# Polynomial attention with 32-row score tiles, lifted scores, a masked diagonal and overlapped units

## Chip, cores and metric

The program runs on one core of one Trainium2 chip. The metric is the device time of one execution, in microseconds (us). The engines are named as in the profile: PE (TensorE matmul), PEld (its weight loads), DVE (VectorE), ACT (ScalarE), POOL (GpSimd), SP.

## What is computed

Two "macaron" layers run over x of shape 4 x 1024 x 128: mixture-of-experts, attention, mixture-of-experts, FFN in one form, then softmax attention and another FFN. The change touches the first attention alone, which has 16 heads of 8 features, a causal mask and, in place of softmax, a polynomial of each score:

```python
qkv = x @ W_attn
att = einsum('bhid,bhjd->bhij', q, k) / sqrt(8)
# for i >= j:  att > 0: (att**2 + 1) / 1000;  -100 <= att <= 0: (1 - 0.01*att) / 1000;  below -100: 0
y = einsum('bhij,bhjd->bhid', polymax(att), v)
x = x + y.reshape(B, T, C) @ W_proj
```

## The kernel before

`macaron` (L2019) runs its phases one after another. Each is a block in which every engine has its own program and waits on semaphores. `attn0_phase` (L886) is the phase that changes.

**Loops.** Batch elements b (4) and in each 4 groups g of 4 heads; m = 4b + g counts the 16 groups. `pipeline` (L976) has each engine do `attend` for group m with `prepare` for group m + 1 threaded in between, so that ten units u of scores alternate with ten steps k of preparation. The loop over the first three elements is a loop on the chip; the last one is written out.

**Layout.** A head takes a strip of 32 rows (`ROW`). Queries and keys are kept as three-part sums in the rows of a strip (high and low halves), so one product in the reduced float32 form (fp32r) gives the full score. `kM` holds four copies of the keys, each with the rows of the other heads zeroed, so each head's score product runs over all 128 rows (L1079).

**Units.** `key_units` (L1424) gives three units for the first 512 queries and seven for the second: 0 and 3 are on the diagonal (four pieces of 128 columns), 1 and 4 have pieces of 384 and 128, 2 and 5 one of 256, and 6 to 9 one of 512. That makes 18 pieces for each of 4 heads.

**A unit.** TensorE makes the scores of each head in one of four PSUM banks; on the diagonal a further product adds a large negative mask (L1083). ScalarE rectifies each head (L1221) and on the diagonal also writes 1 - 0.01 s into `L` (L1220), which GpSimd masks (L1023). VectorE forms r(r + 0.01) in place (L1335); for head 0 of the last three units ScalarE and GpSimd do so (L1225, L1027). TensorE multiplies by the values, four heads at once in 32-column strips, in full float32 (L1098), then adds `L` (L1106) and, for keys further back, a running sum over keys, `S`, applied to the queries (L1112). ScalarE copies the result out (`copy_out`, L1207).

**Preparation.** k = 0, 1 keys; 2 to 5 keys and values by token (`KV`); 6, 7 queries; 8, 9 the running sum. Products go to two banks in turn (L1057, L1063, L1069). ScalarE takes the low halves (L1195) and masks `kM` (L1203); VectorE writes keys, queries and `KV` (L1284 to L1290), `run` (L1301) and the largest magnitudes of keys and queries (L1308, L1315, L1318). GpSimd then makes `S` in three steps (L1007, L1011, L1014).

**The branch.** At a group's end `correct` (L964) has TensorE, ScalarE and VectorE read a flag and branch: only if a score could be under -100 do they recompute the group. It is not taken with this input. After four groups `finish` projects (L1170) and VectorE adds to x with new statistics (L118 to L133).

What sets the order around the change is this hand-written order of each engine, for TensorE:

```python
for u in range(NU):
    scores(m, g, u)
    nxt(u)                      # prepare(m + 1, ..., u)
    if u >= 1:
        values(m, g, u - 1)
```

## Time and profile before

| what | us |
| --- | --- |
| median of 3 runs (3367.14 to 3372.04) | 3371.26 |
| the profiled execution, its own time | 3360.91 |
| its span on the core | 3359.2 |
| PE, DVE, ACT, POOL busy | 2946.4, 2270.8, 1310.0, 858.1 |
| mean granted TensorE clock, share of full speed | 0.935 |

Rows name line, engine, operation and tiles as "out<-in". A group's row ends with count, busy time, mean ns of one instruction, and the engine's idle time just before these with what ended most of it. Line numbers are those of the kernel before. The chain that ended last covers the last few per cent alone (PE 2%, DVE 1%), so stages are read by stretches of time instead.

### The profile page before, as it was taken

Reading aid. Unit: us, or ns where it says so; the run is one execution under the profiler, and the core shown is the slowest. Engines: PE = TensorE matmul, PEld = TensorE weight load, DVE = VectorE, ACT = ScalarE, POOL = GpSimd, SP = SyncE. Lnnn points to the kernel's source line nnn. Section 1 sums busy time; section 2 is a strip of 40 time slices with the busy share of each in tenths; the row PEclk is TensorE's granted clock in tenths of the full one; section 3 lists DMA queues with packets and bytes.
Section 4 is the critical chain, followed back from the end, with each engine's and each line's share of the span. In section 5 each row is a group of like instructions: output and inputs, shape, how many; then the busy total and the mean of one; then the engine's idle time right before and its main releaser. Section 6 shows DMA issues by size and latency. Waiting matters only on the chain. (4 is left out here: it accounts for less than half of the span.)

```text
span 3359.2 us, 58774 instructions
## 1 busy us (share of the span) xinstructions
PE 2946.4 (88%) x16264; PEld 2055.3 (61%) x16296; DVE 2270.8 (68%) x5642; ACT 1310.0 (39%) x2660; POOL 858.1 (26%) x1265
## 2 busy tenths in 40 slices
PE   5999999777777778777999999787998999999987
PEld 4777777655655556555777777644555455565553
DVE  6777777678778677776777777635555555565633
ACT  2111111156566566652111111133554554545532
POOL 1232323244444444441223232101111111111100
PEclk9999999888889988888999999897999999999988
DMA  3000000000000000002000000000000000000000
GB/s 123 0 0 0 0 0 0 1 2 2 3 2 2 3 2 2 2 2 98 0 0 0 0 0 0 1 0 1 1 2 2 1 1 1 1 1 1 1 1 25
DMA packets 13041, 24.09 MB, mean 7 GB/s; under 512 B 2307, under 2 KB 7683, under 8 KB 12805
## 3 DMA queue, kind: packets, MB, share of 16 engines
q1 hardware_dynamic: 12804, 21.22, 1.9%
q8 instruction: 115, 1.88, 0.2%
q14 instruction: 122, 0.99, 0.1%
HBM read 18.52 MB, written 2.10 MB: 6 GB/s over the span
## 5 line engine op out<-in xcount | busy, mean ns | idle before, releaser
L555 DVE SCALAR_TENSOR_TENSOR moe_acc<-moe_ps,moe_comb,moe_acc 128x512 f32<-128x512 f32 x896 | 662.8, 746 | 173.6 <-PE moe_ps L304 170.1
L1335 DVE SCALAR_TENSOR_TENSOR attn_R<-attn_R 128x512 f32<-128x512 f32 (+1 forms) x592 | 479.0, 865 | 116.3 <-ACT attn_R L1221 116.1
L1941 DVE CUSTOM_DVE_ANT_0 attn_masked<-attn_psm,attn_causal 128x1024 f32<-128x1024 f32 (+7 forms) x512 | 367.6, 755 | 205.2 <-PE attn_psm L1666 201.5
L1845 ACT ACTIVATE attn_probs<-attn_pse 128x512 f32<-128x512 f32 (+1 forms) x640 | 319.7, 552 | 291.3 <-PE attn_pse L1680 290.8
L1221 ACT ACTIVATE attn_R<-attn_ps 128x512 f32<-128x512 f32 (+1 forms) x640 | 322.1, 570 | 75.1 <-PE attn_ps L1079 75.1
L304 PE MATMUL moe_ps<-moe_Wg,moe_xh 128*128 128x512 f32 x1024 | 328.9, 403 | 24.2 <-DVE moe_Wu L501 24.2
L304 PE MATMUL moe_ps<-moe_Wu,moe_xh 128*128 128x512 f32 x1024 | 337.0, 411 | 0.0
L335 PE MATMUL moe_ps<-moe_Wd,moe_ih 128*128 128x512 f32 x1024 | 336.4, 410 | 0.0
L1696 PE MATMUL attn_psy<-attn_probs,attn_V 128*64 128x512 f32 (+3 forms) x1536 | 320.7, 517 | 0.4 <-POOL attn_probs L1601 0.3
L1079 PE MATMUL attn_ps<-attn_qS,attn_kM 128*128 128x128 f32 (+3 forms) x1152 | 259.4, 367 | 46.1 <-issue 42.8
L454 POOL TENSOR_SCALAR moe_part<-consts,moe_pick,moe_prob 128x8 f32<-128x8 f32 x256 | 97.4, 394 | 754.1 <-ACT moe_prob L389 754.1
L1601 POOL TENSOR_SCALAR_AFFINE_SELECT attn_probs<-attn_probs 128x256 f32<-128x256 f32 (+1 forms) x192 | 94.7, 493 | 751.3 <-ACT attn_probs L1845 751.3
L1098 PE MATMUL attn_ps<-attn_R,attn_KV 128*32 128x128 f32 (+3 forms) x2304 | 173.8, 417 | 114.1 <-DVE attn_R L1335 113.3
L1079 PEld LDWEIGHTS attn_ps<-attn_qS,attn_kM 128*128 128x128 f32 x1152 | 205.5, 223 | 110.9 <-issue 61.1
L1680 PE MATMUL attn_pse<-attn_qS,attn_kS 110*128 110x512 f32 (+3 forms) x768 | 232.2, 392 | 23.9 <-ACT attn_probs L1845 15.1
L1023 POOL TENSOR_TENSOR attn_L<-attn_L,attn_small 128x512 f32<-128x512 f32 x128 | 206.0, 1639 | 160.9 <-ACT attn_L L1220 160.9
L304 PEld LDWEIGHTS moe_ps<-moe_Wg,moe_xh 128*128 128x128 f32 x1024 | 194.5, 191 | 73.5 <-issue 27.9
L1680 PEld LDWEIGHTS attn_pse<-attn_qS,attn_kS 110*128 110x128 f32 x768 | 119.5, 193 | 188.3 <-ACT attn_probs L1845 109.2
L388 ACT ACTIVATE moe_prob<-moe_gap 128x2 f32<-128x2 f32 x64 | 13.0, 203 | 548.5 <-DVE moe_gap L546 548.5
L335 PEld LDWEIGHTS moe_ps<-moe_Wd,moe_ih 128*128 128x128 f32 x1024 | 185.1, 191 | 41.5 <-issue 1.1
L304 PEld LDWEIGHTS moe_ps<-moe_Wu,moe_xh 128*128 128x128 f32 x1024 | 187.2, 193 | 36.7
L304 PE MATMUL moe_ps<-moe_Wg,moe_xl 128*128 128x512 f32 x512 | 204.7, 400 | 0.0
(207 smaller groups left out, 5033.0 us busy)
## 6 DMA issues: line engine op xcount, KB each, us to landing
moe_stageg<-in_w_gate SPq DMA_DIRECT2D x8, 512.0 KB, 6.9
moe_stageu<-in_w_up SPq DMA_DIRECT2D x8, 512.0 KB, 7.6
moe_stageg<-in_w_down SPq DMA_DIRECT2D x8, 512.0 KB, 3.6
out<-X SPq DMA_DIRECT2D x1, 2048.0 KB, 8.7
attn_qS<-attn_mh SPq DMA_DIRECT2D x64, 4.0 KB
attn_qS<-attn_ml SPq DMA_DIRECT2D x64, 4.0 KB
attn_wd<-in_wd SPq DMA_DIRECT2D x1, 864.0 KB, 5.9
attn_w<-in_wqkv SPq DMA_DIRECT2D x1, 768.0 KB, 5.2
```

The source lines that it names most:

```text
L304: last = pe.matmul(expert_bank[j % 4][:, :], a[q][:, :], w[b][:, cols], start=k == 0, stop=k == 2)
L335: last = pe.matmul(y_bank[h][:, :], a[q][:, rows], W[2][b][:, cols], start=c == 0 and k == 0, stop=c == KC - 1 and k == 2)
L555: dve.scalar_tensor_tensor(acc[:, q, r, :], expert_bank[j % 4][:, :], comb[:, q, r, e:e + 1], acc[:, q, r, :], ALU.mult, ALU.add).then_inc ...
L1023: pool.tensor_tensor(L[:, s, j, :], L[:, s, j, :], seen, ALU.mult).then_inc(g_ready, 1)
L1079: last = pe.matmul(e_bank[j][:, at_:at_ + n], kM[q][:, j, kt * P:(kt + 1) * P], qS[q][:, s * HALF + qc:s * HALF + qc + n], start=not diago ...
L1098: last = pe.matmul(y_bank[rows, qc:qc + n], KV[q][:, kt, P + j * ROW:P + (j + 1) * ROW], R[:, u % 2, j, at_:at_ + n], start=first and k == ...
L1221: act.activation(R[:, u % 2, j, HALF - n:HALF], e_bank[j][:, HALF - n:HALF], ACT.Relu).then_inc(r_ready, 1)
L1335: dve.scalar_tensor_tensor(r, r, -SLOPE, r, ALU.add, ALU.mult).then_inc(u_ready, 1)
L1680: last = pe.matmul(e_bank[c][:, at_:at_ + n], kS[:, kt * P:(kt + 1) * P], qS[q][c][:, s * HALF + qc:s * HALF + qc + n], start=True, stop=True)
L1696: last = pe.matmul(y_bank[VW * c:VW * (c + 1), qc:qc + n], V[:, kt, :], probs[:, u % 2, c, at_:at_ + n], start=first and k == 0, stop=end, ...
L1845: act.activation(probs[:, u % 2, c, HALF - n:HALF], e_bank[c][:, HALF - n:HALF], ACT.Exp, scale=SCORE_SCALE).then_inc(p_ready, 1)
L1941: dve.tensor_tensor_reduce(masked[:, k % 2, 0:n], m_all[:, base:base + n], causal[:, SEQ - n:SEQ], 1.0, NEG, ALU.add, ALU.max, mx[:, q, v: ...
```

## The change

**Scores.** `kM` and its four ScalarE copies per group are gone. A score product takes only its head's 32 rows of `kS` and `qS`, and writes to its own bank: heads 0 and 1 to one of two two-bank tiles `e01`, heads 2 and 3 to the one two-bank tile `e23`. All eight banks are in use, so preparation has one bank (`a_bank`) instead of two. The mask product is gone.

**Lifted scores.** Rows 24 to 26 of a strip add 0.01 to each score s, so that the banks hold t = s + 0.01. Off the diagonal VectorE writes max(t, 0.01) - 0.005 for heads 0 and 1 in one instruction over both (`take`) and then squares it in place; ScalarE does the same for heads 2 and 3 with Relu (`rectify`) and Square. That gives s(s + 0.01) up to a constant which goes into the running sum. The 37 VectorE products, the 3 ScalarE additions and the 3 GpSimd products per group of the old form are gone.

**Diagonal.** VectorE multiplies all four heads' t by the 0/1 mask into `T0` (two instructions), ScalarE writes relu(T0 - 0.01), and VectorE forms (r - 0.01) T0 (two instructions). `L`, its ScalarE copies, its GpSimd masking and its 32 strip products per half are gone; the constant 1 comes from one full-width product per diagonal piece with the fixed tile `seen_one`.

**Order.** `R` has four slots, not two. Each engine starts unit u + 1 (or unit 0 of the next group) before it prepares step u; TensorE multiplies values two units behind. ScalarE does the same order: `rectify` of k + 1, `prepare` k, `square` of k + 1, and `copy_out` of the first half at k = 4. The copying of `KV` moves from VectorE to ScalarE, without its constant columns, which GpSimd writes once at the start. The opening of the next element is done in halves in steps 8 and 9. GpSimd keeps only the three steps of `S`. `finish` writes to `e01[1]`. `correct` keeps its place and its test.

```diff
...
+LIFT = 0.01
+HALF_LIFT = 0.005
...
-        kS = sb("kS", [P, SEQ], F32R)
-        kM = [sb(f"kM{q}", [P, GH, SEQ], F32R) for q in range(2)]
+        kS = [sb(f"kS{q}", [P, SEQ], F32R) for q in range(2)]
         qS = [sb(f"qS{q}", [P, SEQ], F32R) for q in range(2)]
...
-        R = sb("R", [P, 2, GH, HALF])
-        R2 = sb("R2", [P, 2, HALF])
-        L = sb("L", [P, 2, GH, HALF])
+        R = sb("R", [P, SLOTS, GH, HALF])
+        T0 = sb("T0", [P, GH, HALF])
+        seen_one = sb("seen_one", [P, P])
...
+        def slot(q, u):
+            return (2 * q + u) % SLOTS
 
...
+                pool.tensor_scalar(seen_one[:, :], seen[:, 0:P], 1.0 + LIFT * LIFT, None, ALU.mult).then_inc(seen_set, 1)
+                for q in range(2):
+                    pool.tensor_copy(KV[q][:, :, :], kv_ones.unsqueeze(1).to_broadcast([P, BT, 2 * P])).then_inc(kv_set, 1)
...
+                def step(m, g, b, more, has_next):
+                    if has_next:
+                        state(m + 1, (g + 1) % 2)
+                pipeline(pool, lambda: state(0, 0), step, lambda b, more: None)
...
+                def product(out, q, j, s, kt, at_, qc, n):
+                    rows = slice(j * ROW, (j + 1) * ROW)
+                    return pe.matmul(out[:, j % 2, at_:at_ + n], kS[q][rows, kt * P:(kt + 1) * P],
+                                     qS[q][rows, s * HALF + qc:s * HALF + qc + n], start=True, stop=True)
                 def scores(m, g, u):
-                    q = g % 2
                     s, pieces = units[u]
-                    for j in range(GH):
-                        pe.wait_ge(r_ready, after(m * US + (u - 1) * GH + j))
-                        diagonal = pieces[0][4]
-                        for k, (kt, at_, qc, n, _) in enumerate(pieces):
-                            last = pe.matmul(e_bank[j][:, at_:at_ + n], kM[q][:, j, kt * P:(kt + 1) * P],
-                                             qS[q][:, s * HALF + qc:s * HALF + qc + n], start=not diagonal or k == 0,
-                                             stop=not diagonal, skip_group_check=diagonal)
-                        if diagonal:
-                            last = pe.matmul(e_bank[j][:, :], t.identb, t.neg_kq, start=False, stop=True, skip_group_check=True)
-                        last.then_inc(s_ready, 1)
+                    pe.wait_ge(read01, after(m * NU + u - 2))
+                    pe.wait_ge(read23, after(m * NU + u - 1))
+                    for k, (kt, at_, qc, n, _) in enumerate(pieces):
+                        for j in range(GH):
+                            ins = product(e01[u % 2] if j < 2 else e23, g % 2, j, s, kt, at_, qc, n)
+                            if k == len(pieces) - 1 and j == 1:
+                                ins.then_inc(s01_ready, 1)
+                    ins.then_inc(s23_ready, 1)
...
+                    if u in DIAGONAL:
+                        pe.wait_ge(x_ready, after(m * ND + DIAGONAL.index(u)))
+                    else:
+                        pe.wait_ge(sq01_ready, after(m * NO + OTHERS.index(u)))
+                        pe.wait_ge(sq23_ready, after(m * NO + OTHERS.index(u)))
+                    weighted(q, slot(q, u), pieces, first).then_inc(pv_ready, 1)
                     if end:
-                        pe.wait_ge(g_ready, after((m * 2 + s) * GH + GH - 1))
                         for kt, at_, qc, n, _ in key_units(s)[0]:
-                            for j in range(GH):
-                                rows = slice(j * ROW, (j + 1) * ROW)
-                                pe.matmul(y_bank[rows, qc:qc + n], KV[q][:, kt, P + j * ROW:P + (j + 1) * ROW],
-                                          L[:, s, j, at_:at_ + n], start=False, stop=False, skip_group_check=True)
+                            pe.matmul(y_bank[:, qc:qc + n], KV[q][:, kt, P:2 * P], seen_one[:, :], start=False, stop=False,
+                                      skip_group_check=True)
...
+                def step(m, g, b, more, has_next):
+                    for k in range(NU):
+                        if k == 0 and g == 0:
                             pe.wait_ge(res.xo_ready, after(b * 2 - 1))
-                        nxt(u)
-                        if u == 4:
-                            pe.wait_ge(bound_ready, after(m * 3 + 2))
-                            pe.wait_ge(flag_ready, after(m - 1))
-                            pe.matmul(x_bank[0:1, 0:GH], bound[:, g % 2, 2:3], head_mask, start=True, stop=True).then_inc(peak_ready, 1)
-                        if u >= 1:
-                            values(m, g, u - 1)
-                    if more and g == GROUPS - 2:
-                        open_element(b + 1)
-                    values(m, g, NU - 1)
+                        if k + 1 < NU:
+                            scores(m, g, k + 1)
+                        elif has_next:
+                            scores(m + 1, (g + 1) % GROUPS, 0)
+                        if has_next:
+                            if k == 0 and g == GROUPS - 1:
+                                pe.wait_ge(xl_ready, after(b * 2 + 3))
+                            if k == NU - 1 and opens(g, more, k):
+                                pe.wait_ge(xl_ready, after(b * 2 + 2))
+                            if k == 5:
+                                pe.wait_ge(top_ready, after(m))
+                            prepare(m + 1, (g + 1) % GROUPS, k)
+                        if opens(g, more, k):
+                            pe.wait_ge(av_ready, after((m + 1) * NU + k))
+                            open_half(b + 1, k - (NU - 2))
+                        if k >= 2:
+                            values(m, g, k - 2)
+                        if k == 4:
+                            highest(m, g, has_next)
+                    for u in (NU - 2, NU - 1):
+                        values(m, g, u)
                     correct(pe, pe_pause, m, g % 2, lambda: low_scores(m, g), ((cs_ready, US), (cv_ready, NU)))
...
-                    if k in KMASKS:
-                        j = KMASKS.index(k)
-                        if j == 0:
-                            act.wait_ge(av_ready, after(m * NU + 1))
-                            act.wait_ge(s_ready, after((m - 1) * US - 1))
-                        act.activation(kM[g % 2][:, j, :], f32(kS[:, :]), ACT.Copy, scale=head_mask[:, j:j + 1]).then_inc(km_ready, 1)
+                        act.activation(low[:, k % 2, :], a_bank[:, :], ACT.Copy,
+                                       scale=k_low if kind == "k" else q_low).then_inc(t_ready, 1)
+                    elif kind == "kv":
+                        act.wait_ge(ap_ready, after(m * NU + k))
+                        act.wait_ge(y_ready, after((m - 1) * 2 - 1))
+                        act.activation(KV[g % 2][:, 2 * i:2 * i + 2, :].rearrange("p j (g c) -> p (j g) c", c=ROW)[:, :, 0:3 * HD],
+                                       a_bank[:, :].rearrange("p (n c) -> p n c", c=ROW)[:, :, 0:3 * HD],
+                                       ACT.Copy).then_inc(av_ready, 1)
+                def rectify(m, g, u):
+                    n, r = width(u), slot(g % 2, u)
+                    act.wait_ge(pv_ready, after(m * NU + u - SLOTS))
+                    if u in DIAGONAL:
+                        for h in range(2):
+                            act.wait_ge(read23 if h else read01, after(m * NU + u))
+                            act.sem_inc(act_pause, 1)
+                            act.activation(R[:, r, 2 * h:2 * h + 2, :], T0[:, 2 * h:2 * h + 2, :], ACT.Relu,
+                                           bias=minus_lift).then_inc(rd_ready, 1)
+                    else:
+                        act.wait_ge(s23_ready, after(m * NU + u))
+                        act.sem_inc(act_pause, 1)
+                        act.activation(R[:, r, 2:4, HALF - n:HALF], e23[:, :, HALF - n:HALF], ACT.Relu,
+                                       bias=minus_lift).then_inc(read23, 1)
+                def square(m, g, u):
+                    if u in DIAGONAL:
+                        return
+                    n = width(u)
+                    r = R[:, slot(g % 2, u), 2:4, HALF - n:HALF]
+                    act.wait_ge(read23, after(m * NU + u))
+                    act.sem_inc(act_pause, 1)
+                    act.activation(r, r, ACT.Square, bias=half_lift).then_inc(sq23_ready, 1)
 
...
+                def take(m, g, u):
+                    n, r = width(u), slot(g % 2, u)
+                    dve.wait_ge(s01_ready, after(m * NU + u))
+                    if u in DIAGONAL:
+                        some = seen.unsqueeze(1).to_broadcast([P, 2, HALF])
+                        dve.tensor_tensor(T0[:, 0:2, :], e01[u % 2][:, :, :], some, ALU.mult).then_inc(read01, 1)
+                        dve.wait_ge(s23_ready, after(m * NU + u))
+                        dve.tensor_tensor(T0[:, 2:4, :], e23[:, :, :], some, ALU.mult).then_inc(read23, 1)
+                    else:
+                        dve.wait_ge(pv_ready, after(m * NU + u - SLOTS))
+                        dve.sem_inc(dve_pause, 1)
+                        dve.tensor_scalar(R[:, r, 0:2, HALF - n:HALF], e01[u % 2][:, :, HALF - n:HALF], LIFT, -HALF_LIFT,
+                                          ALU.max, ALU.add).then_inc(read01, 1)
+                def square(m, g, u):
+                    if u in DIAGONAL:
+                        return
+                    n = width(u)
+                    r = R[:, slot(g % 2, u), 0:2, HALF - n:HALF]
+                    dve.wait_ge(read01, after(m * NU + u))
+                    dve.sem_inc(dve_pause, 1)
+                    dve.tensor_tensor(r, r, r, ALU.mult).then_inc(sq01_ready, 1)
+                def diagonal(m, g, u):
+                    for h in range(2):
+                        r = R[:, slot(g % 2, u), 2 * h:2 * h + 2, :]
+                        dve.wait_ge(rd_ready, after((m * ND + DIAGONAL.index(u)) * 2 + h))
+                        ins = dve.scalar_tensor_tensor(r, r, -LIFT, T0[:, 2 * h:2 * h + 2, :], ALU.add, ALU.mult)
+                    ins.then_inc(x_ready, 1)
...
+                def step(m, g, b, more, has_next):
+                    for k in range(NU):
+                        if k == 5:
+                            highest(m, g % 2)
+                        if k + 1 < NU:
+                            take(m, g, k + 1)
+                        elif has_next:
+                            take(m + 1, (g + 1) % GROUPS, 0)
+                        if k == 6:
+                            decide(m, g % 2)
+                        if has_next:
+                            prepare(m + 1, (g + 1) % GROUPS, k)
+                        if opens(g, more, k):
+                            low_x(b + 1, k - (NU - 2))
+                        if k + 1 < NU:
+                            square(m, g, k + 1)
+                        if k + 1 in DIAGONAL:
+                            diagonal(m, g, k + 1)
+                        if k == NU - 1 and has_next:
+                            diagonal(m + 1, (g + 1) % GROUPS, 0)
+                        if more and g == GROUPS - 2 and k == NQ0:
                             normalise(b + 1)
-                    if more and g == GROUPS - 2:
-                        open_element(b + 1)
-                    correct(dve, dve_pause, m, g % 2, lambda: low_weights(m, g), ((cc_ready, US), (cm_ready, 2 * GH), (cy_ready, 2)))
...
```

## Rows read from the trace of the kernel before

**Rows 1.** The page's first part: busy time, share, instructions of each engine

```profile
PE 2946.4 (88%) x16264; PEld 2055.3 (61%) x16296; DVE 2270.8 (68%) x5642; ACT 1310.0 (39%) x2660; POOL 858.1 (26%) x1265
```

**Rows 2.** Stretches: length, busy of PE, PEld, DVE, ACT, POOL, granted clock, DMA

```profile
674.90:1515.20 840.30, 653.49 (x5800) 478.66 (x5832) 655.08 (x1030) 516.16 (x982) 375.87 (x224) 0.88 0.01 2
...
1050.40:1057.20 6.80, 6.80 (x25) 6.16 (x27) 4.09 (x3) 4.59 (x9) 4.54 (x3) 0.50 0.00 0
...
1074.00:1091.00 17.00, 13.26 (x93) 7.50 (x91) 16.90 (x31) 15.14 (x28) 3.88 (x3) 1.00 0.01 1
```

**Rows 3.** Order of time: start, us; yS copies that end groups 0 and 12

```profile
737.50 0.60 ACT L1207 ACTIVATE attn_yS<-attn_ps 128x512 f32<-128x512 f32 x1 [5.06 <-PE attn_ps L1112]
...
1361.91 0.60 ACT L1207 ACTIVATE attn_yS<-attn_ps 128x512 f32<-128x512 f32 x1 [5.28 <-PE attn_ps L1112]
```

**Rows 4.** VectorE's groups in the phase: count, busy us, mean ns, idle before

```profile
L1335 DVE SCALAR_TENSOR_TENSOR attn_R<-attn_R 128x512 f32<-128x512 f32 x464 | 433.6, 990 | 116.3 <-ACT attn_R L1221 116.1
L1335 DVE SCALAR_TENSOR_TENSOR attn_R<-attn_R 128x256 f32<-128x256 f32 x128 | 45.4, 415 | 0.0
L1290 DVE TENSOR_TENSOR attn_KV<-attn_ps,attn_small 128x512 f32<-128x512 f32 x60 | 40.8, 680 | 0.0
L1301 DVE TENSOR_TENSOR attn_run<-attn_ps,attn_run 128x128 f32<-128x128 f32 x106 | 30.5, 288 | 2.6
L1287 DVE SCALAR_TENSOR_TENSOR attn_qS<-attn_ps,attn_small,attn_low 128x512 fp32r<-128x512 f32 x30 | 22.3, 743 | 0.0
...
L1315 DVE TENSOR_REDUCE attn_bound<-attn_qS 128x1 f32<-128x1024 f32 x16 | 19.3, 1205 | 0.0
...
L1318 DVE SCALAR_TENSOR_TENSOR attn_bound<-attn_bound,attn_small 128x1 f32<-128x1 f32 x16 | 10.3, 642 | 0.0
...
L118 DVE TENSOR_TENSOR attn_xo<-attn_ps,X 128x512 f32<-128x512 f32 x8 | 5.5, 692 | 51.7 <-PE attn_ps L1170 51.7
```

**Rows 5.** Order of time: VectorE's products with GpSimd beside them, and alone

```profile
1052.66 6.33 POOL L1023 TENSOR_TENSOR attn_L<-attn_L,attn_small 128x512 f32<-128x512 f32 x4 [4.47 <-ACT attn_L L1220]
1053.11 6.44 DVE L1335 SCALAR_TENSOR_TENSOR attn_R<-attn_R 128x512 f32<-128x512 f32 x4 [8.47 <-ACT attn_R L1221]
...
1079.05 2.49 DVE L1335 SCALAR_TENSOR_TENSOR attn_R<-attn_R 128x512 f32<-128x512 f32 x4
```

**Rows 6.** GpSimd's groups in the phase

```profile
L1023 POOL TENSOR_TENSOR attn_L<-attn_L,attn_small 128x512 f32<-128x512 f32 x128 | 206.0, 1639 | 160.9 <-ACT attn_L L1220 160.9
...
L1014 POOL TENSOR_TENSOR attn_S<-attn_runm,attn_runl 128x1024 fp32r<-128x1024 f32 x16 | 37.9, 2366 | 1.3
L1007 POOL TENSOR_TENSOR attn_runm<-attn_run,attn_small 128x1024 f32<-128x1024 f32 x16 | 37.7, 2357 | 63.7 <-DVE attn_run L1301 63.7
L1011 POOL TENSOR_TENSOR attn_runl<-attn_runm,attn_small 128x1024 fp32r<-128x1024 f32 x16 | 30.3, 1892 | 2.9 <-POOL attn_runm L1007 2.9
```

**Rows 7.** Order of time, TensorE: idle before in brackets, PEld loads weights

```profile
1050.39 2.31 PE L1079 MATMUL attn_ps<-attn_qS,attn_kM 128*128 128x128 f32 x8 [2.87 <-issue]
...
1060.61 0.54 PEld L1079 LDWEIGHTS attn_ps<-attn_qS,attn_kM 128*128 128x128 f32 x4 [0.20 <-issue]
...
1067.47 1.06 PE L1106 MATMUL attn_ps<-attn_L,attn_KV 128*32 128x128 f32 x32
...
1081.59 1.07 PE L1098 MATMUL attn_ps<-attn_R,attn_KV 128*32 128x512 f32 x8 [0.55 <-DVE attn_R L1335]
...
1082.59 1.20 PE L1079 MATMUL attn_ps<-attn_qS,attn_kM 128*128 128x512 f32 x4
```

**Rows 8.** Single lines: count, duration ns min/median/max; then two ScalarE groups

```profile
L501 DVE TENSOR_TENSOR moe_Wg<-moe_stageg,moe_Wg x8: 1214/1216/1226, 22.5 to 1549.2; 128x1024 fp32r<-128x1024 f32 x8
...
L1941 DVE CUSTOM_DVE_ANT_0 attn_masked<-attn_psm,attn_causal x512: 276/756/1226, 2294.6 to 3191.0; 128x1024 f32<-128x1024 f32 x22, 128x256 f32<-128x256 f32 x22, 128x640 f32<-128x640 f32 x22, 128x128 f32<-128x128 f32 x21
...
L1221 ACT ACTIVATE attn_R<-attn_ps 128x512 f32<-128x512 f32 x512 | 283.3, 615 | 27.6 <-PE attn_ps L1079 27.6
...
L1203 ACT ACTIVATE attn_kM<-attn_kS,attn_small 128x1024 fp32r<-128x1024 f32 x60 | 71.1, 1184 | 0.0
```

362 lines of the change are left out of this document (170 added, 192 removed).

## The prediction

> **What bounds the kernel now.** The page's totals name TensorE [rows 1], but the change touches one phase, so I read that phase by stretches first. It lasts 840.3 us from its first products to its last sums; in it VectorE is busy 655 us, TensorE 653, ScalarE 516 and GpSimd 376 [rows 2]. No engine is full over the phase. Between the ends of groups 0 and 12 lie 1361.91 - 737.50 = 624.4 us [rows 3], so 52.0 us a group and 208 us an element.
>
> The stretches tell two situations apart. In the middle of a group VectorE is busy 16.90 of 17.00 us and TensorE 13.26 [rows 2]: there VectorE bounds. At a group's opening it is not VectorE: its first product of a group came after 8.47 us of idleness [rows 5], and such waits, on ScalarE's rectified scores, are 116.3 us in all, 7.3 a group [rows 4]. What ScalarE waits for is TensorE, which after the branch at a group's end stood 2.87 us [rows 7] and then made the diagonal scores at clock 0.50, the 1.2 GHz level [rows 2].
>
> VectorE's busy time is itself swollen. Four products took 6.44 us beside four masking steps of GpSimd that took 6.33, but 2.49 us, 0.62 each, with GpSimd at rest [rows 5]: the two take turns. The wide products have a mean of 990 ns and 479.0 us in all [rows 4]; at 0.62 us for 29 a group and 0.35 for 8 they would be 20.8 x 16 = 333 us. So 146 us, 9 a group, are turns lost to GpSimd.
>
> **VectorE after, a group.** Every new instruction spans 1024 columns. The nearest rows give 1.22 us for a two-input operation in SBUF and 1.23 for the widest with a PSUM input [rows 8]; I take 1.21, and for 512 columns 0.68 [rows 4].
> - Reading scores: 4 for the two diagonals and 6 wide, 10 x 1.21, and 2 x 0.68: 13.5 us.
> - Squares: 6 x 1.21 + 2 x 0.68 = 8.6 us.
> - Diagonal products: 4 x 1.21 = 4.8 us.
> - Preparation: keys and queries 4 x 0.743, running sum 7 x 0.29 with its chain 2.3, two maxima 2.4, bound and flag 0.9: 8.6 us. `KV` (4 x 0.68 = 2.7 us) has left for ScalarE.
>
> Sum 35.5 us, where before the same sum is 20.8 + 11.3 = 32.1 clean and 41 with the turns. So VectorE gets more work, not less; the gain must come from turns and idleness.
>
> Turns: of GpSimd's 24 us a group only the three steps of `S` stay, 2.36 + 1.89 + 2.37 = 6.6 us [rows 6]. They start when the running sum is done, exactly when VectorE comes to the next diagonal's two products, which read SBUF twice. Each waits behind one step: 2.36 + 1.89 = 4 us. Bounds: 0 if they fall beside readings of PSUM, 6.6 if all three are met.
>
> Waits: in four steps (0, 1, 6, 7) VectorE needs ScalarE's low half, which comes after TensorE's product (3 x 0.23) and ScalarE's rectification; about 0.5 us each, 2 us. A square right behind its own reading waits for it to land, 0.15 us, four times: 0.6. The branch leaves 0.3 us uncovered. The opening wait of 7.3 us goes, since scores of unit 0 are made in the old group's last step, before the branch, and what VectorE meets there are its own diagonal products. Added up a plain group takes 42.4 us. Followed step by step through the four engines' orders, where a wait can fall inside a turn, it comes to 39.5, and to 41 where TensorE's low level reaches into it; I take 40.
>
> **Per element** come `normalise` and the opening of x (4 us of VectorE) and `finish`: the projection, 64 products at the 1.2 GHz level, then the residual, near 12 us. Before, the wait for the projection was 51.7 us over 8 [rows 4], and it stays. An element is 4 x 40 + 16 = 176 us against 208.
>
> **TensorE after, a group**, at full clock. A weight load of 128 columns follows the last by 0.11 us (four in 0.54 with the last one's own 0.19), and four 32-column strips run together (32 products in 1.06 us) [rows 7]. If 32-row tiles do so too, a piece costs its columns once for four heads: 18 pieces, 2.6 us, where one unit of four heads now takes 1.20 us [rows 7] and a group about 14 with masks. Preparation 7.2, values 7.9 (a wide unit 0.88), ones and `S` 2.6, thirty changes of tile shape at the 0.20 us idle seen at one [rows 7] 6, branch 2.9: 29 us. With 7 us of these at the low level 32 to 33. That is under 40, so it is covered by VectorE; if VectorE were faster, this would be next.
>
> On those changes of shape there is a rule against the edit. The Trainium skill (TensorEngine Tiling (Array Packing), Key Properties) says that a change of tiling mode drains TensorE, and the new order has three shapes in a unit instead of two. Here a change shows as 0.20 us of idle load queue [rows 7], and ten more of them are 2 us a group, inside the cover. By the rule with a drain as long as a wide product's 0.4 us it would be 4 us, still inside it.
>
> **ScalarE after**: rectifying and squaring of two heads, 1.1 us for 1024 columns (0.615 for 512, plus a pointer operand) against 1.18 with a pointer scale [rows 8]: 12 x 1.1 + 4 x 0.7, diagonal 4 x 1.13, low halves 2.9, `KV` 4 x 0.5, copies 1.2, branch 0.7: 27 us. Covered. A chain through it is new: `e23` has no second buffer, so scores of u + 1 wait for the rectification of u. Scores 0.5 plus 1.1 are 1.6 us against VectorE's 3.2 in a wide step: covered. The one bank of preparation likewise makes step k + 1 wait for VectorE's or ScalarE's evacuation of k, one step earlier.
>
> **The sum.** Three elements save 32 us each, 96. The last one, whose final group has nothing to prepare, and the start together save about 13. That is 109, and I take off 4 for the queues' handling of the added pauses: 105 us. The profiled execution's 3360.91 (span 3359.2) becomes 3256. It stands 10.4 us below the median of the three runs, 3371.26, so the median becomes 3266 us.
>
> **Rivals.**
> - *Tiles run one by one.* If each 32-row product pays its own load, the scores cost 72 x 0.11 to 0.23 us, 10 instead of 2.6, and TensorE reaches 38 to 40 us a group. Element 183 us, gain 80 to 90: 3285. For it: full-height loads follow one another at 0.11 us [rows 7]. Against: the strips of 32 columns do. Chance 0.14. The Trainium skill (TensorE: Matmul & The Clock Gate, LDWEIGHTS) holds that a load costs by its columns whatever its rows, while its packing part lets loads of different row groups overlap; no row here has a 32-row tile.
> - *VectorE meets more turns and waits.* All three steps of `S` met (6.6), each pause and own wait 0.3 us on twenty instructions (+5), the evacuation chain showing in kv steps: 46 to 48 us a group, gain 40 to 60, 3320. Chance 0.16.
> - *TensorE stays at the low clock* (the slower side). Place: the matrix products of a plain group. TensorE has 26 us to work in 40 (29 less the branch), and the trace has the level at 0.50 after each gap like the 2.87 us one. If it stays at 1.2 GHz, 2 x 26 + 3 = 55 us a group against 52 now, and more where VectorE's waits add: 20 to 140 us slower, middle 3440. It decides from the point where low-level work makes TensorE's 29 us exceed 52, nearly the whole group. Against: a TensorE that falls behind at the low level is then never idle, and at such a place, fully busy for 6.80 us at 0.50, the level came back [rows 2]. Chance 0.06.
> - *The change does little*, the overlap being undone by the order, for instance by the peak product that VectorE awaits at step 5 holding the shared bank: 50 to 52 us a group, 3360 to 3375. Chance 0.03.
> - *More than that*: turns vanish and waits hide, 36.8 us a group, gain 135 to 150: 3230. Chance 0.10.
>
> My forecast keeps 0.51.
>
> **Numbers.** The likeliest case gives 3266, own range 3245 to 3280. The range for 8 in 10 takes in the small side, the serial tiles and most of the turns case: 3218 to 3330; it leaves out the slow clock, no effect, and the tails. A change of 0.2%, 7 us, is about what a measurement of this kernel can tell from none. Faster by more: 0.51 + 0.14 + 0.16 + 0.10, less 0.01 of the turns case's tail, 0.90. Within: 0.02 of the little-effect case. Slower: the clock case's 0.06, 0.01 of the little-effect case and that 0.01, 0.08.
>
> **What would show it.** Right: groups of 40 us with VectorE over 90% busy in them; its squares and readings 1.2 us; the diagonal products showing 2 us and more beside GpSimd's `S` and 1.2 elsewhere; four score products of a piece starting within a few hundredths of a us; TensorE near 60 to 70% with its low level short. Wrong: score products a full load apart (serial tiles); `take` waiting for TensorE; the clock at 0.50 through groups; VectorE's idle time in front of keys and queries over 1 us each.

## The result

| | us |
|---|---|
| before, median of 4 runs | 3370.05 (3367.14 to 3372.04) |
| after, median of 4 runs | 3234.57 (3233.32 to 3239.37) |
| ratio | 0.9601, 95% interval 0.9585 to 0.9618 |
| profiled execution after: time, span | 3233.72, 3231.8 |

The kernel is 135.5 us faster by the medians and 127.4 by the two profiled spans (3359.2 to 3231.8). I had forecast 3266, 105 us less. First the phase by stretches, after; its columns are those of [rows 2]. The first row answers to the 840.30 us there, the other four are the groups of the second element, cut at ScalarE's `yS` copies.

```profile
679.80:1382.00 702.20, 537.42 (x4936) 342.80 (x4936) 600.51 (x758) 404.37 (x486) 139.18 (x48) 0.81 0.01 2
...
868.90:918.30 49.40, 36.75 (x355) 25.63 (x355) 42.76 (x64) 24.84 (x31) 8.10 (x3) 0.86 0.01 3
918.30:957.20 38.90, 32.06 (x291) 19.84 (x291) 35.17 (x41) 25.10 (x32) 9.48 (x4) 0.78 0.01 2
957.20:1007.20 50.00, 38.36 (x299) 22.62 (x299) 42.52 (x52) 26.20 (x33) 15.28 (x6) 0.69 0.01 2
1007.20:1041.20 34.00, 28.57 (x291) 18.05 (x291) 30.53 (x38) 24.86 (x30) 1.33 (x2) 0.90 0.01 2
```

The same four groups of the kernel before:

```profile
887.40:945.10 57.70, 44.07 (x409) 33.86 (x411) 42.27 (x79) 31.69 (x62) 20.75 (x14) 0.94 0.01 3
945.10:993.50 48.40, 37.70 (x345) 27.11 (x347) 38.91 (x57) 32.07 (x61) 24.56 (x16) 0.89 0.01 2
993.50:1047.60 54.10, 41.14 (x353) 30.09 (x355) 42.34 (x67) 33.46 (x64) 26.77 (x16) 0.84 0.01 2
1047.60:1095.60 48.00, 38.34 (x345) 27.59 (x347) 38.91 (x57) 32.08 (x62) 20.57 (x14) 0.89 0.01 2
```

The phase is 138.1 us shorter; 10.7 us are lost again outside this stretch, 4.9 ahead of its first products and 5.8 behind its end; the cause stays open. The element takes 172.3 us against 208.2. VectorE is busy 600.51 of 702.20 us, 86%, where it was 78%; GpSimd's 376 us have become 139. The first row of an element's four holds the projection of the last element, the third the opening of the next. The second is a plain group. The fourth looks short (34.0 us, 38 VectorE instructions against 41) because of where it is cut: unit 0 of that group was begun before the `yS` copy at 1007.22, so VectorE's two diagonal products and nearly all of GpSimd's steps stand in the third row. A plain group is better read where neither neighbour is cut so. Two of the last element:

```profile
1260.85:1297.66 36.81, 29.05 (x291) 18.12 (x291) 34.88 (x41) 24.88 (x32) 9.39 (x4) 0.86 0.01 2
1297.66:1336.20 38.54, 30.79 (x291) 19.07 (x291) 35.04 (x41) 24.90 (x32) 9.38 (x4) 0.82 0.01 2
```

With 749.08 to 786.01, 918.30 to 957.16 and 1090.71 to 1127.67 there are five such stretches, 188.1 us together: 37.6 us a plain group, in which VectorE is busy 35.0 us (93%) and TensorE 30.1 (80%). Before, the two plain groups shown take 48.2 us in the mean. TensorE's clock is lower than before, 0.81 for 0.88 in the mean of the phase.

VectorE's groups in the phase, after (columns as in [rows 4]):

```profile
L1366 DVE TENSOR_TENSOR attn_R<-attn_R 128x1024 f32<-128x1024 f32 x96 | 118.7, 1237 | 5.2
L1356 DVE TENSOR_SCALAR attn_R<-attn_e 128x1024 f32<-128x1024 f32 x96 | 116.9, 1218 | 18.7 <-PE attn_e L1059 12.5 <-issue 6.2
L1372 DVE SCALAR_TENSOR_TENSOR attn_R<-attn_R,attn_T 128x1024 f32<-128x1024 f32 x64 | 109.1, 1745 | 2.8 <-ACT attn_R L1215 2.8
...
L1350 DVE TENSOR_TENSOR attn_T<-attn_e,attn_small 128x1024 f32<-128x1024 f32 x32 | 38.9, 1216 | 0.7 <-PE attn_e L1059 0.7
...
L1311 DVE SCALAR_TENSOR_TENSOR attn_qS<-attn_a,attn_small,attn_low 128x512 fp32r<-128x512 f32 x32 | 23.9, 747 | 18.7 <-ACT attn_low L1199 18.7
L1306 DVE SCALAR_TENSOR_TENSOR attn_kS<-attn_a,attn_small,attn_low 128x512 fp32r<-128x512 f32 x32 | 23.9, 746 | 18.7 <-ACT attn_low L1199 18.6
...
L118 DVE TENSOR_TENSOR attn_xo<-attn_e,X 128x512 f32<-128x512 f32 x8 | 5.5, 688 | 12.7 <-PE attn_e L1173 12.7
```

The opening wait of 116.3 us [rows 4] is gone: the reading that opens a group (L1350) waits 0.7 us in all. What VectorE still waits for is ScalarE's low halves (18.7 + 18.7 us), scores off the diagonal (18.7 us ahead of L1356) and the projection, 12.7 us where it was 51.7 [rows 4].

A change of groups in order of time, VectorE and GpSimd only:

```profile
952.50 1.21 DVE L1366 TENSOR_TENSOR attn_R<-attn_R 128x1024 f32<-128x1024 f32 x1
...
953.63 1.22 DVE L1350 TENSOR_TENSOR attn_T<-attn_e,attn_small 128x1024 f32<-128x1024 f32 x1
...
954.77 1.21 DVE L1352 TENSOR_TENSOR attn_T<-attn_e,attn_small 128x1024 f32<-128x1024 f32 x1
...
955.90 0.93 DVE L1324 TENSOR_TENSOR attn_run<-attn_a,attn_run 128x128 f32<-128x128 f32 x3
...
956.75 0.21 DVE L1334 SCALAR_TENSOR_TENSOR attn_bound<-attn_bound,attn_small 128x1 f32<-128x1 f32 x1
956.87 4.51 DVE L1372 SCALAR_TENSOR_TENSOR attn_R<-attn_R,attn_T 128x1024 f32<-128x1024 f32 x2
957.00 3.30 POOL L1007 TENSOR_TENSOR attn_runm<-attn_run,attn_small 128x1024 f32<-128x1024 f32 x1 [29.14 <-DVE attn_run L1324]
...
960.48 2.65 POOL L1011 TENSOR_TENSOR attn_runl<-attn_runm,attn_small 128x1024 fp32r<-128x1024 f32 x1 [0.18 <-POOL attn_runm L1007]
961.30 1.21 DVE L1356 TENSOR_SCALAR attn_R<-attn_e 128x1024 f32<-128x1024 f32 x1
```

Two things are to be seen. The two diagonal products take 4.51 us beside GpSimd's step, which takes 3.30 where 2.36 was its mean before [rows 6]: the turn predicted, and it costs both sides. It is one turn, not two. The first product of this pair took 1.22 us and the second 3.37, and in 15 of the 16 groups the first is within 1.21 to 1.22 and the second within 2.9 to 3.4. And an operation of 1.21 or 1.22 us is followed by the next after 1.13 and 1.14 us: neighbours on VectorE overlap by 0.08 us, so durations added up say too much.

```profile
L1372 DVE SCALAR_TENSOR_TENSOR attn_R<-attn_R,attn_T x64: 1210/1225/3401, 710.3 to 1349.6; 128x1024 f32<-128x1024 f32 x64
```

The middle duration of all 64 is 1225 ns: most of these products meet no turn.

Four score products of one piece, TensorE, at full clock:

```profile
1030.66 0.19 PEld L1059 LDWEIGHTS attn_e<-attn_qS,attn_kS 32*128 32x128 f32 x4 [0.41 <-issue]
1030.67 0.50 PE L1059 MATMUL attn_e<-attn_qS,attn_kS 32*128 32x512 f32 x4
```

Four heads' loads take 0.19 us together, where four full-height ones took 0.54, and the four products 0.50 for 1.20 [rows 7]. The 32-row tiles run side by side. The Trainium skill (TensorEngine Tiling (Array Packing), Key Properties) says that different tiles can load and multiply in parallel; the rows agree.

### The profile page after: what moved, and what is told of

Its sections match the earlier page's. It is cut to its first block and busy times, and to the rows that moved or that the text cites. A ratio compares the mean times of both kernels' runs of the same rounds, so it can differ in the third digit from the quotient of the medians.

```text
span 3231.8 us, 55337 instructions
## 1 busy us (share of the span) xinstructions
PE 2837.1 (88%) x15400; PEld 1923.0 (60%) x15400; DVE 2216.7 (69%) x5370; ACT 1198.5 (37%) x2164; POOL 628.1 (19%) x1092
## 5 line engine op out<-in xcount | busy, mean ns | idle before, releaser
L304 PE MATMUL moe_ps<-moe_Wu,moe_xl 128*128 128x512 f32 x512 | 204.5, 399 | 0.0
L335 PE MATMUL moe_ps<-moe_Wd,moe_il 128*128 128x512 f32 x512 | 203.2, 397 | 0.0
L1744 PE MATMUL attn_psm<-attn_kS,attn_qS 108*128 108x512 f32 (+3 forms) x672 | 178.5, 371 | 15.7 <-DVE attn_mx L2019 15.3
L1077 PE MATMUL attn_y<-attn_R,attn_KV 128*32 128x128 f32 (+3 forms) x2304 | 179.4, 446 | 1.3 <-DVE attn_R L1366 1.2
L1744 PEld LDWEIGHTS attn_psm<-attn_kS,attn_qS 108*128 108x128 f32 x672 | 120.7, 196 | 56.6 <-DVE attn_mx L2019 37.7
L1356 DVE TENSOR_SCALAR attn_R<-attn_e 128x1024 f32<-128x1024 f32 (+1 forms) x128 | 138.7, 1084 | 22.1 <-PE attn_e L1059 15.9
```

Source lines behind the costliest of these rows:

```text
L304: last = pe.matmul(expert_bank[j % 4][:, :], a[q][:, :], w[b][:, cols], start=k == 0, stop=k == 2)
L335: last = pe.matmul(y_bank[h][:, :], a[q][:, rows], W[2][b][:, cols], start=c == 0 and k == 0, stop=c == KC - 1 and k == 2)
L1077: last = pe.matmul(y_bank[rows, qc:qc + n], KV[q][:, kt, P + j * ROW:P + (j + 1) * ROW], R[:, r, j, at_:at_ + n], start=first and k == 0, ...
L1356: dve.tensor_scalar(R[:, r, 0:2, HALF - n:HALF], e01[u % 2][:, :, HALF - n:HALF], LIFT, -HALF_LIFT, ALU.max, ALU.add).then_inc(read01, 1)
L1744: last = pe.matmul(m_all[:, base + lo:base + hi], qS[q][c][0:STACK, j * P:(j + 1) * P], keys[0:STACK, lo:hi], start=True, stop=True)
```

## The experiments

Twelve kernels (the last four under one heading). Each ratio is against runs of the kernel before made beside it, with its 95% interval. To set them against the change I take 0.9601 for it and 3370 us for one; such differences are good to some 7 us. Line numbers shift by a few between kernels.

**1. GpSimd's masks and products nearly taken away, in the kernel before.**

```diff
-pool.tensor_tensor(L[:, s, j, :], L[:, s, j, :], seen, ALU.mult).then_inc(g_ready, 1)
+pool.tensor_tensor(L[:, s, j, 0:8], L[:, s, j, 0:8], seen[:, 0:8], ALU.mult).then_inc(g_ready, 1)
...
-r = R[:, u % 2, 0, HALF - width(u):HALF]
-pool.tensor_tensor(r, r, R2[:, u % 2, HALF - width(u):HALF], ALU.mult).then_inc(up_ready, 1)
+r = R[:, u % 2, 0, HALF - 8:HALF]
+pool.tensor_tensor(r, r, R2[:, u % 2, HALF - 8:HALF], ALU.mult).then_inc(up_ready, 1)
```

ScalarE's copy into `L`, not shown here, writes a constant.

> The kernel before, with GpSimd's masking steps and its three products a group cut to 8 columns, and the low-side term set to a constant (so that term and part of the products of one head are left out). Theory: the turns with GpSimd are on VectorE's path. The wide products fall from a mean of 990 ns to about 570, VectorE's busy time in the phase from 655 to about 510 us, and the kernel from 3370 to 3290 (3270 to 3310); the opening wait of 7.3 us a group stays. Rival: the opening chain (branch, scores, rectification) and TensorE set the group, and the turns only fill idle time: less than 20 us. If it falls to 3235 alone, the turns were the whole gain of the change.

Measured 0.9686 (0.9667 to 0.9704), 106 us faster, more than the 60 to 100 expected.

```profile
L1335 DVE SCALAR_TENSOR_TENSOR attn_R<-attn_R 128x512 f32<-128x512 f32 x464 | 303.1, 695 | 145.9 <-ACT attn_R L1221 144.9
L1335 DVE SCALAR_TENSOR_TENSOR attn_R<-attn_R 128x256 f32<-128x256 f32 x128 | 45.5, 418 | 0.0
```

Against [rows 4] the products lose 130.5 us, and their opening wait grows from 116.3 to 145.9. The mean of 695 ns is not the 570 I expected: I had mixed the two widths, and 0.62 us is the distance between products, not the duration of one. The turns were on VectorE's path. But the work itself is left out here too, so the next kernel was needed.

**2. The same work moved to VectorE**, in the kernel before:

```diff
-        POOLED = range(NU - 3, NU)
+        POOLED = range(0)
...
+                        for j in range(GH if pieces[0][4] else 0):
+                            dve.wait_ge(l_ready, after(m * 2 * GH + (GH if u else 0) + j))
+                            lj = L[:, units[u][0], j, :]
+                            dve.tensor_tensor(lj, lj, seen, ALU.mult).then_inc(g_ready, 1)
```

> The kernel before, with GpSimd's masking steps and its three products a group moved to VectorE (nothing is left out). VectorE then has 39 us of work a group, none of it in turns but beside the state's steps. Theory: the turns cost more than the work itself: with 7 us of opening wait a group takes 46 us, and 3370 becomes 3275 to 3300. Rival: the masks on VectorE delay its products and with them TensorE: 3330 or more.

Measured 0.9937 (0.9920 to 0.9954), 21 us faster. The theory missed. The time lies where the rival put it (3330 or more).

```profile
L1329 DVE SCALAR_TENSOR_TENSOR attn_R<-attn_R 128x512 f32<-128x512 f32 x512 | 328.7, 689 | 144.8 <-ACT attn_R L1215 141.2 <-issue 2.8
L1333 DVE TENSOR_TENSOR attn_L<-attn_L,attn_small 128x512 f32<-128x512 f32 x128 | 79.7, 683 | 0.0
L1329 DVE SCALAR_TENSOR_TENSOR attn_R<-attn_R 128x256 f32<-128x256 f32 x128 | 45.4, 414 | 0.0
```

VectorE's products and masks together are 453.8 us, only 25 less than the 479.0 of before with the turns in it [rows 4]. Against the 348.6 us of the last experiment the moved work adds 105, nearly the 130.5 that the turns had cost. The wait ahead of the products grows too, from 116.3 to 144.8 us. That part fits the rival, but its way through TensorE is not shown: TensorE's wait for these products fell from 113.3 to 90.9 us. (My 46 us a group also left out what an element adds to its four groups, which the 52.0 of before contains.) So moving the work would have brought a sixth of the gain. The new form has no low-side term to mask and leaves the squares of two heads to ScalarE; it does not hand the work on to VectorE. How much of the gain each of these is worth, and what the wider instructions and the four slots add, no run takes apart.

**3. The 32-row tiles alone**, in the kernel before (two buffers of `kS`, no `kM`):

```diff
-last = pe.matmul(e_bank[j][:, at_:at_ + n], kM[q][:, j, kt * P:(kt + 1) * P],
-                 qS[q][:, s * HALF + qc:s * HALF + qc + n], start=not diagonal or k == 0,
+last = pe.matmul(e_bank[j][:, at_:at_ + n], kS[q][j * ROW:(j + 1) * ROW, kt * P:(kt + 1) * P],
+                 qS[q][j * ROW:(j + 1) * ROW, s * HALF + qc:s * HALF + qc + n], start=not diagonal or k == 0,
...
-                    if k in KMASKS:
+                    if False:
```

> The kernel before, with score products on 32-row tiles of the keys in place of the four masked copies of them (the same values come out). Theory: TensorE saves little, since each head waits for its own bank, and ScalarE saves four copies of 1024 columns a group, near 4 us of 32; neither bounds the middle of a group: 3370 becomes 3345 to 3370. Rival: the tiles are a large part of the gain by themselves: 3330 or less.

Measured 0.9994 (0.9979 to 1.0010): nothing. Its phase by stretch:

```profile
674.90:1517.00 842.10, 689.26 (x5832) 431.89 (x5832) 644.48 (x1023) 454.13 (x918) 369.85 (x224) 0.80 0.01 2
```

ScalarE is busy 62 us less than in [rows 2] and it changes nothing. TensorE has shorter score products and is yet busy 36 us more, at a mean clock of 0.80 instead of 0.88: the projections of queries and keys, which the edit leaves alone (L1057), take 567 ns in the mean instead of 475.

**4. Unit 0 of a group begun after the branch**, in the changed kernel (so on all four engines):

```diff
                 def step(m, g, b, more, has_next):
+                    scores(m, g, 0)
...
-                        elif has_next:
-                            scores(m + 1, (g + 1) % GROUPS, 0)
```

> The changed kernel, with unit 0 of a group begun after the branch instead of before it. Theory: the overlap across groups is worth what the opening wait cost before, 4 to 7 us a group, and it also covers the wait for the projection: 3235 becomes 3300 to 3345, and VectorE's wait ahead of the residual sum rises from 12.7 to about 50 us. Rival 1: the wait for the projection has shrunk for another reason, and stays near 13 us. Rival 2: the overlap is worth little, less than 20 us, and turns and instruction counts made the gain.

Measured 0.9733 (0.9714 to 0.9752), 44 us slower than the changed kernel, under the expected 65 to 110.

```profile
L1368 DVE SCALAR_TENSOR_TENSOR attn_R<-attn_R,attn_T 128x1024 f32<-128x1024 f32 x64 | 79.6, 1285 | 5.2 <-ACT attn_R L1213 5.2
L1346 DVE TENSOR_TENSOR attn_T<-attn_e,attn_small 128x1024 f32<-128x1024 f32 x32 | 39.1, 1222 | 67.4 <-PE attn_e L1059 61.6 <-issue 5.8
...
L118 DVE TENSOR_TENSOR attn_xo<-attn_e,X 128x512 f32<-128x512 f32 x8 | 5.5, 692 | 40.0 <-PE attn_e L1171 40.0
```

The opening wait is back, 67.4 us or 4.2 a group, where the theory said 4 to 7, and so is most of the wait for the projection, 40.0 where it said about 50. What made the undoing cheaper is the first row: the diagonal products fall from 1745 to 1285 ns, 29.5 us, since they no longer stand beside GpSimd's state steps. So the overlap across groups is paid for in part with those turns.

**5. The state's steps cut to one block of eight**, changed kernel:

```diff
-pool.tensor_tensor(runm[:, :, :], run[:, :, :], state_mask.unsqueeze(1).to_broadcast([P, BT, P]),
+pool.tensor_tensor(runm[:, c, :], run[:, c, :], state_mask.unsqueeze(1).to_broadcast([P, c.stop - c.start, P]),
```

> The changed kernel, with GpSimd's three steps for the state of the running sum cut from eight key blocks to one (the other seven of the state keep the first group's value, so that part of the result is left out). Theory: their turns with VectorE lie on its path: the diagonal products fall from a mean of 1745 ns to about 1230, 2.1 us a group, and the kernel from 3235 to 3203 (3195 to 3220). Rival: VectorE then only waits elsewhere, and the gain is under 8 us.

Measured 0.9598 (0.9573 to 0.9623): not to be told from the changed kernel, at most some 10 us.

```profile
L1375 DVE SCALAR_TENSOR_TENSOR attn_R<-attn_R,attn_T 128x1024 f32<-128x1024 f32 x64 | 82.3, 1328 | 2.8 <-ACT attn_R L1218 2.8
...
L1309 DVE SCALAR_TENSOR_TENSOR attn_kS<-attn_a,attn_small,attn_low 128x512 fp32r<-128x512 f32 x32 | 24.0, 750 | 28.7 <-ACT attn_low L1202 28.4
...
L118 DVE TENSOR_TENSOR attn_xo<-attn_e,X 128x512 f32<-128x512 f32 x8 | 5.5, 692 | 24.0 <-PE attn_e L1176 24.0
```

The rival fits: the profiled span is 8 us shorter, the ratio no different. The turns are gone (26.8 us of the diagonal products), and VectorE waits instead: 10 us more before keys, 11.3 more for the projection. At a change of groups something other than the turns comes last.

**6. The branch left out**, changed kernel:

```diff
-            may_be_low = eng.value_load(flag[0:1, q:q + 1], min_val=0, max_val=1)
-            with eng.If(may_be_low):
...
-            with eng.Else():
-                for s, n in totals:
-                    eng.sem_inc(s, n)
+            for s, n in totals:
+                eng.sem_inc(s, n)
```

> The changed kernel, without the branch at a group's end (the second way for very low scores is left out; the wait for the flag stays). Theory: TensorE's chain through the branch and the low clock after it bound the change of groups: 20 to 45 us off, 3190 to 3215, and the mean clock in the phase rises from 0.81 to 0.9 or more. Rival, as predicted: VectorE covers all but 0.3 us a group: 3228 to 3235.

Measured 0.9541 (0.9525 to 0.9557), 20 us faster or 1.3 a group, at the edge of the theory. TensorE's wait ahead of the next keys, with the branch (first) and without:

```profile
PE attn_a L1043 <- DVE attn_kS L1306: 35.3, 16, 5.3
```

```profile
PE attn_a L1037 <- DVE attn_kS L1300: 52.4, 16, 5.3
```

The phase without:

```profile
680.00:1360.00 680.00, 526.90 (x4931) 336.27 (x4930) 592.20 (x752) 402.31 (x485) 141.36 (x48) 0.81 0.01 1
```

The clock did not rise, 0.81 as before: that part of the theory falls. TensorE reaches the preparation sooner, and waits there for VectorE to empty the shared bank, 52.4 us against 35.3 with the branch. I read the branch and this wait as two parts of one idle stretch.

**7. Every score product three times**, changed kernel:

```diff
-                    for k, (kt, at_, qc, n, _) in enumerate(pieces):
+                    for k, (kt, at_, qc, n, _) in enumerate(pieces * 3):
...
-                            if k == len(pieces) - 1 and j == 1:
+                            if k == len(pieces) * 3 - 1 and j == 1:
```

> The changed kernel, with every score product made three times into the same place (the result stays). That is 36 more pieces a group, 5.2 us at full clock. Theory: TensorE has slack in the middle of a group and none at its change, so 5 to 30 us slower: 3240 to 3265. Rival 1: TensorE sets the whole group: 80 us or more slower. Rival 2: more work keeps its clock up (0.81 over the phase now), and the time stays or falls. If the tiles run side by side, four 512-wide products again take 0.50 us, three times over.

Measured 0.9703 (0.9682 to 0.9724), 34 us slower, just past the 5 to 30 of the theory.

```profile
1041.04 0.98 PE L1059 MATMUL attn_e<-attn_qS,attn_kS 32*128 32x512 f32 x12
```

```profile
L1350 DVE TENSOR_TENSOR attn_T<-attn_e,attn_small 128x1024 f32<-128x1024 f32 x32 | 39.1, 1221 | 13.9 <-PE attn_e L1059 13.8
```

Twelve products take 0.98 us where four took 0.50, so a further set of four costs 0.24. Of TensorE's added work 2.1 us a group show, less than half of the 5.2. VectorE's diagonal readings now wait 13.9 us for scores where it was 0.7, and the wide readings (L1356) 39.2 where it was 18.7: TensorE's slack no longer covers them. The clock is 0.83 in the phase, hardly higher; rival 2 falls.

**8. Elements 1 to 3 not opened** (they use the first one's transposed input), changed kernel: `opens` returns False, and `normalise(b + 1)` is left out.

> The changed kernel, with elements 1 to 3 using the first element's transposed input, so that normalising, transposing and splitting x in the third group of an element are left out. Theory: this opening costs 9 to 13 us an element through its chain over the one shared bank: 3235 becomes 3197 to 3210. Rival, as predicted: only VectorE's 4 us an element: 3220 to 3226.

Measured 0.9519 (0.9503 to 0.9535), 28 us faster, 9.2 us for each of three openings: within the theory's 9 to 13, and not my predicted 4. VectorE is busy 585.0 us in the phase instead of 600.5, so 5.2 of each 9.2 are its own work. In the changed kernel it also waits ahead of the subtraction that ends an opening, 10.3 us in all:

```profile
L1297 DVE TENSOR_TENSOR attn_xT<-attn_a,attn_xT 128x512 fp32r<-128x512 f32 x8 | 5.5, 692 | 10.3 <-ACT attn_xT L1192 10.3
```

**9 to 12. Squares moved from VectorE to ScalarE**, changed kernel. For the units in `MOVED` ScalarE adds, behind its own square, one for heads 0 and 1, and VectorE skips it:

```diff
+                    if u in MOVED:
+                        r = R[:, slot(g % 2, u), 0:2, HALF - n:HALF]
+                        act.wait_ge(read01, after(m * NU + u))
+                        act.activation(r, r, ACT.Square).then_inc(sqa_ready, 1)
...
-                    if u in DIAGONAL:
+                    if u in DIAGONAL or u in MOVED:
```

Units 4 and 7:

> The changed kernel, with the squares of heads 0 and 1 of units 4 and 7 made by ScalarE. VectorE has 2.5 us a group less of its 37.5, ScalarE 2.3 more of 25. Theory: VectorE bounds the middle of a group, and TensorE with its branch and low clock bounds the change of groups, so part of it shows: 3235 becomes 3205 to 3222. Rival 1: VectorE bounds throughout: 40 us off, 3195. Rival 2: VectorE isn't the bound: within 5 us of 3235.

Measured 0.9636 (0.9618 to 0.9653), 12 us slower. No theory had that sign. Its query operations, and then the same line with units 4, 8 and 9:

```profile
L1319 DVE SCALAR_TENSOR_TENSOR attn_qS<-attn_a,attn_small,attn_low 128x512 fp32r<-128x512 f32 x32 | 24.1, 752 | 43.0 <-ACT attn_low L1203 43.0
```

```profile
L1319 DVE SCALAR_TENSOR_TENSOR attn_qS<-attn_a,attn_small,attn_low 128x512 fp32r<-128x512 f32 x32 | 23.9, 747 | 18.0 <-ACT attn_low L1203 18.0
```

Unit 7's square is queued at the end of step 6. Only one rectification stands between it and the low half of the queries of step 7, and VectorE waits 24 us more for that. It also waits 14 us more for scores, against some 32 us of work that it is rid of.

Units 4, 6, 8 and 9:

> As the last, with units 4, 6, 8 and 9: VectorE down 5 us a group to near 32.5, ScalarE up 4.6 to near 30. Theory: 3190 to 3212, and VectorE's idle time ahead of keys and queries and scores grows by 1 to 2 us a group. Rival: ScalarE's squares delay its rectification of heads 2 and 3 and so the scores after them: slower than with two units, or than 3235.

Measured 0.9543 (0.9524 to 0.9562), 20 us faster than the changed kernel, as the theory said.

Units 4, 8 and 9:

> The changed kernel, with the squares of heads 0 and 1 of units 4, 8 and 9 made by ScalarE, and none in the steps ahead of the low halves of the queries. Theory: what made two moved units slower was unit 7's square, which stands in ScalarE's queue ahead of the low half that VectorE waits for; without it VectorE's idle time before its query operations is back near 19 us in all, and the kernel takes 3195 to 3214, under four moved units. Rival: the loss came from elsewhere (the squares falling into GpSimd's turn): 3216 or more.

Measured 0.9510 (0.9494 to 0.9526), 31 us faster. That is one square fewer moved than in the last, and 11 us better by the ratios (6 by the medians), little more than the differences are good to. The wait ahead of the queries is what the theory asked for, 18.0 us, where units 4, 6, 8 and 9 leave 34.2: here no moved square stands right ahead of a low half of the queries.

Units 2, 4, 5, 8 and 9:

> The changed kernel, with the squares of heads 0 and 1 of units 2, 4, 5, 8 and 9 made by ScalarE: against units 4, 8 and 9 alone VectorE loses 1.5 us a group more and ScalarE gains 1.3. Both half-wide squares stand behind the low halves of their steps. Theory: VectorE is busy 536 of 677 us with three units moved, and what is left of the group is set by TensorE's change of groups as much as by it: 3200 to 3210. Rival: VectorE still bounds the middle: 3185 to 3195. Other rival: ScalarE's queue delays the scores: 3215 or more.

Measured 0.9465 (0.9450 to 0.9480), 3190.5 us, 46 us under the changed kernel and the fastest of all.

```profile
680.00:1337.00 657.00, 519.64 (x4936) 336.41 (x4935) 523.28 (x678) 460.96 (x566) 137.19 (x48) 0.83 0.01 2
```

VectorE is down 77 us against the changed kernel's phase and ScalarE up 57. My theory put this at 3200 to 3210 and the rival at 3185 to 3195. The rival is right: VectorE still bounded the middle of a group.

## Why the prediction was right in its mechanism and small in its size

**The mechanism held.** The turns with GpSimd and the opening wait were what held the kernel (experiments 1 and 4), VectorE is the bound after (93% busy in plain groups; experiment 12), the four heads' tiles run side by side, and the clock, though lower, did not stay low. The rivals of serial tiles and of a TensorE left at its low level fall by the profile after. The time lies inside the wide range, 3218 to 3330, but outside the 3245 to 3280 that I gave the likeliest case and beside the 3230 of the rival "More than that", with a chance of 0.10. The reason given there, that turns vanish and waits hide, is only half of it: plain groups take 37.6 us where it said 36.8, and the rest of the gain lies elsewhere.

**VectorE's sum.** From the rows above, a group, as durations:

| | predicted | after |
|---|---|---|
| readings | 13.5 | 13.5 |
| squares | 8.6 | 8.9 |
| diagonal products with turns | 8.8 | 6.8 |
| preparation | 8.6 | 8.3 |
| waits for the low half | 2.0 | 2.3 |

The step that failed is "Each waits behind one step: 2.36 + 1.89 = 4 us". Only one of the two products waited: the turns measured 2 us a group, 1745 ns less the 1237 of the squares, four times. In the change of groups shown the pair lost 2.25 us (4.51 less twice 1.13), about one step of 2.36. And even these are mostly covered (experiment 5). The Trainium skill (SBUF — State Buffer, Summary: rules for kernel authors) says that when a VectorE instruction has two SBUF inputs and the GpSimd one reads SBUF, the second to issue is blocked until the first is done. The rows at 956.87 agree, and GpSimd's steps grew to 8.7 us a group from the 6.6 I carried over.

A second fault is in the same sum: for the kernel before I took 0.62 us from 2.49 us for four products [rows 5], a distance between starts, and for the kernel after 1.21 us from durations of single operations [rows 8]. Those include the 0.08 us of overlap. The first four terms measured add up to 37.5 us, where VectorE is busy 35.0 in a plain group, so 2.5 us a group were counted that do not exist. The 146 us of turns that I read in the kernel before, with 0.62 us as the time of a product alone, were also too many: experiment 1 shows 130.5.

The terms of the prediction add up to 42.4 us. Less the 2 us of turns and the 2.5 of overlap that is 37.9, near the 37.6 measured. My own 40 stood between the two because I had taken 2.4 us off the sum for waits that fall inside turns. That came near by luck: it made up for half of two faults that I had not seen. One term was too small: the branch, put at 0.3 us a group, costs 1.3 (experiment 6).

**Per element.** "Before, the wait for the projection was 51.7 us over 8 [rows 4], and it stays" is wrong: it fell to 12.7, because VectorE has the next group's unit 0 in hand meanwhile, and rose to 40.0 when that was undone. The term of 12 us was still near: the group with the projection takes 49.4 us, 11.8 more than a plain one. The term for the opening, 4 us of VectorE's work, was mis-sized: it costs 9.2, of which 5.2 are VectorE's work and the rest waits; the transposes, ScalarE's copy and VectorE's subtraction follow one another through one shared bank. So 4 x 40 + 16 = 176 came out as 172.3, of which four plain groups are 150.4: 9.6 us too much for the groups and 5.9 too little for the element, in part cancelling.

**The ends.** "Three elements save 32 us each" and 13 for start and last element: the middle two saved 72.7 together, the first and the last 23.4 and 42.0. The last element's groups save 10 us each, as plain groups do elsewhere, and I gave them almost nothing. Against the forecast that is 8.7 + 20.4, and the 4 us taken off for added pauses do not show; less the 10.7 lost outside the phase this is 127.4 for 105. By the medians it is 135.5, since the profiled execution of before stood 9 us under the median of its four runs and the one of after 1 us.

**TensorE and ScalarE.** 29 to 33 us was predicted for TensorE and plain groups show it busy 30.1 in the mean; ScalarE 27 against 25. As a share that is 80%, where my sign of being right was 60 to 70%. Both are covered in the middle of a group. What I did not see is that at a change of groups TensorE's branch, its wait for the shared bank and VectorE's wait for the low half seem to form one chain: when the turns or the branch are taken away, the wait beside them grows (experiments 5 and 6).

## What to carry over

Before moving work off a shared resource, price the work where it would go: turns that look like pure loss can be nearly as long as the work itself, and then only dropping it gains much (106 us dropped, 21 moved). Add up VectorE's time from distances between starts, in both kernels alike. Cut stretches at a mark that every engine passes at the same place of a group, and count the instructions in each. When squares or copies are shared out between engines, the place in the other queue matters more than the count: two moved squares lost 12 us, three in better places gained 31.

## What was not expected of the hardware

Neighbouring VectorE operations of 1.21 to 1.22 us start 1.13 us apart. With shorter score products alone, TensorE's mean clock in the phase fell from 0.88 to 0.80 and the time stayed; but tripling the score products raised it only from 0.81 to 0.83, and leaving out the branch not at all. What moves it here stays open.
